# Storing the queries untransposed and reading them with a transposing DMA, with their rounding one half later and their products in four PSUM banks

## What is computed

```python
def _L0_xattn_ref(x, context, Wq, Wk, Wv):      # x is the layer-normed input, NHEADS = 32, HEAD_DIM = 32
    q = x @ Wq.T
    k_raw = context @ Wk.T
    v_raw = context @ Wv.T
    q = q.reshape(b, n, NHEADS, HEAD_DIM).transpose(0, 2, 1, 3)
    kv = jnp.concatenate([k_raw, v_raw], axis=-1).reshape(b, m, NHEADS, HEAD_DIM, 2)
    k, v = kv[..., 0].transpose(0, 2, 1, 3), kv[..., 1].transpose(0, 2, 1, 3)
    q, k = _rmsnorm(q), _rmsnorm(k)             # t * rsqrt(mean(t * t) + 1e-6) over the 32 of a head
    attn = softmax(einsum('bhnd,bhmd->bhnm', q, k) * HEAD_DIM ** -0.5)
    return einsum('bhnm,bhmd->bhnd', attn, v).transpose(0, 2, 1, 3).reshape(b, n, 1024)

x = x + tanh(g_xattn[0]) * _L0_xattn_ref(_layernorm(x), ctx_2048, Wq, Wk, Wv)
x = x + tanh(g_ffn[0]) * _L0_ffn_ref(_layernorm(x), w1, w2, w3)   # sigmoid(x Q(w1)') * (x Q(w2)'), then Q(w3)'
```

## Time and profile before

| | us |
|---|---|
| median of 3 runs (2406.19 to 2409.27) | 2406.49 |
| time of the profiled execution | 2409.68 |
| its span in the profile | 2407.9 |
| PE busy in the span | 2338.2 (97%) |
| DVE busy | 1423.5 (59%) |
| ACT busy | 1373.6 (57%) |
| POOL busy | 895.3 (37%) |

### The profile page before, as it was taken

The page is one execution under the profiler, slowest core; times in us unless marked ns, Lnnn a source line. Parts: engine busy times, 40 slices in busy tenths (PEclk is TensorE's granted clock), DMA queues, the critical chain, the costliest instruction groups (busy, mean ns, idle before and its releaser), DMA issues.

```text
span 2407.9 us, 46736 instructions
## 1 busy us (share of the span) xinstructions
PE 2338.2 (97%) x17618; PEld 1367.3 (57%) x17618; DVE 1423.5 (59%) x2346; ACT 1373.6 (57%) x2894; POOL 895.3 (37%) x857
## 2 busy tenths in 40 slices
PE   7998899999999999999999999889999999999999
PEld 5885465566656566666666565555555555544444
DVE  5666677776776777777767767664353444410000
ACT  4875787788888888888888888751111111110000
POOL 3664255565655656565656556430000000000000
PEclk9999999999999999999999999999999999999999
DMA  7785544465535445544545454554232323244351
GB/s 244 232 271 172 139 114 99 104 129 100 125 93 124 106 102 125 113 102 113 131 100 124 93 100 105 129 159 125 94 114 95 114 95 104 79 136 147 103 166 53
DMA packets 383233, 299.16 MB, mean 124 GB/s; under 512 B 276512, under 2 KB 338464, under 8 KB 382496
## 3 DMA queue, kind: packets, MB, share of 16 engines
q1 hardware_dynamic: 383008, 296.17, 46.8%
HBM read 196.22 MB, written 49.55 MB: 102 GB/s over the span
## 4 chain that ended last, share of the span: by engine, by line
PE 33%; POOL 29%; issue 26%; DVE 1%; DMA 1%; POOLq 1%; ACT 1%; DVEq 0%; SPq 0%; ACTq 0%
PE ps L1447 21%; POOL krs L707 14%; PE ps L1563 11%; POOL oinv L725 5%; POOL kms L702 4%; POOL osum L723 2%; POOL osum L730 2%; POOL oinv L727 1%; POOL ca L737 1%; POOL cn L751 1%; POOLq L60 0%; POOL crs L747 0%; DMA wraw<-in_wffn 0%; ACT pf L958 0%; DMA stage<-x_normalised 0%
## 5 line engine op out<-in xcount | busy, mean ns | idle before, releaser
L1479 PE MATMUL ps<-wk,cpair 128*128 128x512 f16 x4608 | 1116.5, 379 | 15.1 <-DVE cpair L1086 7.6
L1274 DVE TENSOR_TENSOR plo<-pf,phi 125x448 f16<-125x448 f32 x768 | 526.9, 687 | 160.8 <-ACT phi L949 158.4
L1479 PEld LDWEIGHTS ps<-wk,cpair 128*128 128x128 f16 x4608 | 393.7, 97 | 392.6 <-DVE cpair L1086 8.7
L958 ACT ACTIVATE pf<-ps 125x448 f32<-125x448 f32 x768 | 417.6, 544 | 145.1 <-PE ps L1501 137.1
L1447 PE MATMUL ps<-xnTh,w12q 128*128 128x512 f16 (+1 forms) x1408 | 478.9, 354 | 2.9 <-issue 2.1
L1447 PE MATMUL ps<-xnTl,w12q 128*128 128x512 f16 (+1 forms) x1408 | 478.6, 353 | 0.0
L949 ACT ACTIVATE phi<-pf 125x448 f16<-125x448 f32 x768 | 445.5, 580 | 8.5
L707 POOL TENSOR_TENSOR krs<-kms,mhalf 125x8 f32<-125x8 f32 x192 | 331.4, 1726 | 15.1
L702 POOL TENSOR_TENSOR kms<-kss,keps 125x8 f32<-125x8 f32 x192 | 95.5, 497 | 556.3 <-DVE kss L1240 556.3
L1525 PE MATMUL ps<-val,phi 125*128 125x65 f16 x3072 | 279.6, 192 | 18.9 <-DVE plo L1274 18.8
L1501 PEld LDWEIGHTS ps<-qT,kst 128*125 128x125 f16 x1536 | 209.2, 138 | 144.9
(11 more groups left out here) (113 smaller groups left out, 2461.0 us busy)
## 6 DMA issues: line engine op xcount, KB each, us to landing
gbuf<-in_wffn SPq DMA_DIRECT2D x66, 512.0 KB, 5.0
wraw<-in_wffn SPq DMA_DIRECT2D x66, 512.0 KB, 5.7
cstream<-in_ctx SPq DMA_DIRECT2D x48, 500.0 KB, 4.6
craw<-in_ctx SPq DMA_DIRECT2D x48, 500.0 KB, 4.6
hid<-hidden SPq DMA_DIRECT2D x7, 2816.0 KB, 12.7
hidden<-hh SPq DMA_DIRECT2D x66, 256.0 KB, 2.1
qT<-q_pairs SPq DMA_DIRECT2D x256, 56.0 KB, 2.2
wkraw<-in_wkv SPq DMA_DIRECT2D x4, 2048.0 KB, 8.9
```

The source lines that it names most:

```text
L958: act.activation(pf[0:KW, e % 6, :], bank(3 + e % 3)[0:KW, 0:2 * S], ACT.Exp, bias=LN128, scale=SCALE).then_inc(p_ready, 1)
L1274: dve.tensor_tensor(plo[0:KW, e % 6, :, :], pf[0:KW, e % 6, :].rearrange("p (t n) -> p t n", t=2), phi[0:KW, e % 6, :, :], ALU.subtract).t ...
L1479: mm = pe.matmul(bank(pt)[:, :], cpair[:, n % RING, a, kc, :], wkp[g][:, w, kc, :], start=(kc == 0 and m == 0), stop=(kc == KC - 1 and m = ...
```

## The change

- Q is stored untransposed, in `q_stacked` [token, head, 4, 32], with each head's high part twice and its low part twice. `half_high` and `half_low` therefore write 1024 elements for each row where they wrote 512, through a broadcast of `qhat`.
- `q_stack`, both `half_out` and the buffer `qTs` are gone. `save_q(h)` is one DMA of 512 KB straight from `qnat`. It waits for `qlo_ready`, and `half_high(h)` now waits for the DMA of half h - 2 (`q_saved`).
- `load_qT` is one transposing DMA from DRAM for each unit, 224 rows by 1024.
- `half_high(h)` stands behind `half(h + 1)` on ACT, `half_norm(h)` at the head of half h + 1 on DVE. `ctx_high(0)` stands behind `half(27)` and `half_high(26)`, `ctx_low(0)` behind `half_sums(27)` and `half_low(26)`. On SP `save_q(h)` stands in half h + 1, and so `save_q(0)` stands ahead of the third and fourth `cstream` loads.
- The products of half h go to bank (2, 3, 4, 6)[h % 4], and `q_half(h)` waits for `qhat_ready` of half h - 4.

```diff
+        def q_bank(h):
+            return (2, 3, 4, 6)[h % 4]
...
+            def save_q(h):
+                i, c = h // 2, h % 2
+                sp.wait_ge(qlo_ready, h + 1)
+                sp.dma_start(q_d[i * P:i * P + P, 16 * c:16 * c + 16, :, :].rearrange("t h a d -> t (h a d)"),
+                             qnat[:, c, :, :, :].rearrange("p h a d -> p (h a d)")).then_inc(q_saved[c], 16)
...
-                for i in range(4):
-                    for s in range(2):
-                        r0 = HD2 * s + DH * (i // 2)
-                        sp.dma_start(qT[DH * i:DH * i + DH, par, s:HG:2, :],
-                                     qst_d[g, :, r0:r0 + DH, b * S:b * S + S].rearrange("p r t -> r p t")
-                                     ).then_inc(q_in[par], 16)
+                sp.dma_start_transpose(qT[:, par, :, :], q_d[b * S:b * S + S, HG * g:HG * g + HG, :, :].rearrange(
+                    "t h a d -> t (h a d)")).then_inc(q_in[par], 16)
...
             def half_high(h, c):
                 act.wait_ge(qhat_ready, h + 1)
-                wait(act, qT_ready, h - 1)
-                act.activation(qnat[:, c, :, 0, :], qhat[:, :, :], ACT.Copy).then_inc(qhi_ready, 1)
+                wait(act, q_saved[c], 16 * (h // 2))
+                act.activation(qnat[:, c, :, 0:2, :], qhat[:, :, :].unsqueeze(2).to_broadcast([P, 16, 2, DH]), ACT.Copy
+                               ).then_inc(qhi_ready, 1)
...
                     half(h, c)
-                    if not first:
-                        half_out(h - 2, i - 1, c)
+                    if h:
+                        half_high(h - 1, 1 - c)
+                    if h == 2 * NT - 1:
+                        act.wait_ge(csc_ready, 1)
+                        ctx_high(0)
...
+                    if h:
+                        half_norm(h - 1, 1 - c)
+                    half_sums(h)
+                    if h:
+                        half_low(h - 1, 1 - c)
                     if h == 2 * NT - 1:
                         ctx_low(0)
...
             def q_half(h, i, par, c, first):
                 pe.wait_ge(xlo_ready, i + 1)
-                wait(pe, qhat_ready, h - 1)
+                wait(pe, qhat_ready, h - 3)
```

95 lines of the change are left out of this document (22 added, 73 removed).

## The result

| | before | after |
|---|---|---|
| median, us (lowest to highest) | 2407.26 (2406.19 to 2409.27, 4 runs) | 2385.66 (2383.76 to 2388.80, 4 runs) |
| profiled execution, its span | 2409.68, 2407.9 | 2383.76, 2381.9 |
| ratio of the times, 95% interval | | 0.9911 (0.9893 to 0.9928) |

The change is worth 21.6 us; 21.3 were forecast. The two profiles lie 26.0 us apart, since the profiled execution of before took 2.4 us more than its median and that of after 1.9 us less. They serve for the parts, and the medians for the sum. By the interval the medians' difference is uncertain by about 4 us.

The account below looks back on a forecast made before the run. PE was taken to bound the kernel. Terms 13.2 + 0.5 + 5.2 + 0.7 - 2.4 + 4.1 = 21.3 us, from 2406.49 to a forecast of 2385.2 us; range 2380.5 to 2393.5.

Parts of the forecast that it names:

- start, with the earlier x tile: Start of stage A: half 2 unstalled by four banks, x tile 2's transpose 5.2 us earlier, plus 0.7 for earlier x DMA.
- rest of stage A (13.2 + 0.5 - 2.4): Stage A: 13.2 us from removed stacks, 0.5 from a half no longer waiting for qhat, 2.4 lost before two weight sums.
- between the stages: From half 27 to the key tiles: second key tile earlier, low clock falling on the first key tile, 4.1 us gained.
- The stacks: Stage A: PE loses 25 stacks, 12 x 0.46 + 13 x 0.59 = 13.2 us; the tile becomes 11.75 us.
- ACT's and DVE's growth: Stage A: rounding grows to about 1.03 us, remainder to about 1.22; both fit, costed at zero outside tiles 3 and 9.
- The weight squares: Tiles 3 and 9: ACT's squares end late, PE waits 1.5 us instead of 0.3 before each weight sum, 2.4 us lost.
- The banks: Four banks for Q's products: no wait for qhat at the start, and 0.5 us for one later half.
- the banks do nothing: Rival at the start: xn of tile 2 comes later still, 5.9 us less gain, 2391; chance within another bound's 0.22.
- Stage B at zero: Stage B: one DMA for Q instead of 8 in each unit, unseen by PE, so no gain or loss.
- The transposing read: Stage B's read of Q from DRAM: 2.2 us to issue, 5.4 to landing, scaled from the key transpose.
- The rival of another bound in stage A: ACT, DVE or late DMAs hold most tiles at 12.3 us, or the clock falls: 2392; chance 0.22, banks' case included.
- sign of being wrong: Listed signs: tile near 12.8 us, PE waiting for xlo or xn, ACT waiting for q_saved, reads landing after 10 us.

Follow-up runs that it names:

- experiment 8: The kernel before, with each unit's first gate tile loaded ahead of the eight reads of Q on SyncE; 2397.53 us, 0.9956 of before.
- experiment 2: The changed kernel with eight dummy transposes of the identity into an unused bank behind each half in stage A; 2396.24 us, 0.9952 of before.
- experiment 3: The changed kernel with the squares of the two weight groups spread over more halves; 2381.47 us, 0.989 of before.
- experiment 1: The changed kernel with Q's products in two banks again, each half waiting for qhat of half h - 2; 2394.85 us, 0.995 of before.
- the repetition: The changed kernel run and profiled again, nothing altered, beside the kernel before; 2385.75 us, 0.991 of before.
- Experiments 6 to 9: Experiment 6: the changed kernel with 30 extra transposing reads of Q, ahead of the needed ones, 2397.81 us; experiment 7, experiment 8 and experiment 9 have their own lines.
- experiment 7: The changed kernel with 30 extra transposing reads of Q, each behind the needed read and the unit's first gate tile; 2384.88 us, 0.9906 of before.
- experiment 11: The changed kernel with spread squares, new step order between the stages, first gate tile ahead of Q, and clearing and tables ahead of half 27's norm; 2374.27 us.
- experiment 9: The changed kernel, with each unit's first gate tile loaded ahead of the transposing read of Q; 2380.57 us, 0.9889 of before.
- experiment 5: The kernel before, with the norm of half 0 ahead of the statistics of x tile 2 on DVE; 2404.21 us, 0.9988 of before.

## Why the prediction was right, and where only its sum was

| part of the sum | predicted us | in the two profiles |
|---|---|---|
| start, with the earlier x tile | 5.9 | 6.0 (40.85 to 34.88) |
| rest of stage A (13.2 + 0.5 - 2.4) | 11.3 | 8.6 (half 27 ends at 188.95, before at 203.54) |
| between the stages | 4.1 | 3.8 (to the first score) |
| stage B | 0 | 6.0 |
| behind stage B | 0 | 1.6 |
| sum | 21.3 | 26.0 |

**The start** was right in its steps: half 2 without a wait at full clock, and `xn` next in line with 0.64 us of idle time. It survived a first half that ran 0.94 us later in this execution (x transpose at 22.28). That the size fits so well is luck. The profile of before had a slow start, 2.3 us slower than experiment 8 with the same stage A, so the gain is 3.7 us against that one. The 0.7 us for an earlier x tile are not shown: its statistics stand at 29.62 instead of 30.35, but at 29.12 in experiment 8.

**The stacks** were right. The tile is 11.78 us against 11.75, and experiment 2 gives 1.05 us a tile. ACT's and DVE's growth was right too, 1053 and 1226 ns against 1.03 and 1.22 us, and outside the weight tiles PE shows no wait that comes from it.

**The weight squares** were under-sized. The mechanism was named, at 1.5 us a wait; the waits were 1.65 and 2.15, and the clock fell behind the second, which made the tile 1.7 us longer. I had taken from the earlier trace rows that the clock holds behind 2.46 us of idle. That the second wait is the longer one is the DMA of Q, which ACT waits for in that tile, 0.69 us; in the first such tile ACT idled 0.28 us there, for `qhat`. In all the term is 2.5 us short (0.15 + 0.65 + 1.7), and experiment 3 gets 4.2 back.

**The banks** were right at the start and wrong elsewhere. The text gave them the start's gain and 0.5 us; experiment 1 gives 9.1, of which 6.5 lie in stage A in the profiles, since a half without stacking comes back to its bank before `qhat` is ready. The rival "the banks do nothing" was far off. The sum didn't suffer, because it assumed PE unhindered in the tiles.

**Between the stages** the forecast of the first key product (4.3 us behind half 27, measured 4.24) was right, and that of the second key tile (12.3) became 12.8. The clock was low on the first key tile, as expected: 24 products in 7.04 us (8.1 in the text) in a stretch of 0.81. The 4.1 us of this term came out as 3.8 in the two profiles and as 1.7 in the repetition, whose clock fell once more, behind `khat`.

**Stage B at zero was wrong**, and this is the step that failed: "Between no change (bound below) and one unit's stall (above) I take zero". Two things were missing. One is the bound: eight issues replaced by one free SyncE for the rest of its list, 3.91 us against 1.56 ahead of the gate tiles of the fifth unit, so a gain was possible. The other is what stands behind the read on SyncE. I named the key transposes, not the gate tiles, though the waits view of before has DVE waiting 15.6 us for them. Experiments 6 to 9 show this, and the last two give its size: the gain of the changed kernel over before falls from 21.6 us to 17.0 (2397.53 against 2380.57) once both load the first gate tile ahead of Q. Stage B says the same in the profiles: 6.0 us shorter without that move and 1.4 with it (1321.0 against 1319.6). So about 4.6 us of the medians' 21.6 come from SyncE's list, and 17 from stage A and the passage between the stages, where 21.3 were forecast. The medians alone would not carry this split, since each of these differences is uncertain by 3 to 4 us. Two errors of about 4.5 us cancelled, and that the sum came within 0.3 us is luck.

**The transposing read** lands its 14 blocks in 4.9 us, 0.35 us a block, close to the estimate of 5.4 us. The estimate from the Trainium skill, page VectorE: DVE Perf Modes, The three transpose paths, was 18.3 us for it; this trace does not agree. Issue took 1.57 us against 2.2 estimated, and in experiment 7 30 more such reads cost nothing that the medians show.

The rival of another bound in stage A did not come, beyond the two waits for squares. But one sign of being wrong that the text names did: ACT waited for `q_saved`. DMA ran at a share of about 1.0 from 120 to 145 us in the changed kernel, and what came late in it was neither x nor context but the stored Q; through ACT's full list it reached PE at the second weight sum.

## What to carry to other kernels

A DMA costs its place in the issuing queue even if nobody waits for its data: read what stands behind it, and which engine's list waits for that. A wait of an engine that feeds the bound can cost its whole length though the bound's own gap right behind it shows less than half. It need not (the last one of experiment 8 cost 3.4 of 4.9 us), so compare the spacing of one repeated instruction ahead of the wait and far behind it. When a tile of the bound gets shorter, follow every chain that closes in it again (a bank, a sum of squares), for one that had slack before will now wait.

## What the hardware showed that I had not expected

The clock's fall does not follow the length of the idle time alone. Before the second weight sum PE idled 2.15 and 2.09 us in the two profiles of the changed kernel, and the eight transposes behind ran at about the lower level, 1.2 of 2.4 GHz (1.92 and 1.95 us instead of 1.03). Behind 2.93 us (experiment 1, half 2) PE kept the upper one, with a granted clock of 1.00. Even the same wait ends both ways. Behind 2.92 us for `khat` the next 54 products took 11.83 us at a clock of 1.00 in experiment 2, and 13.39 us at 0.88 in experiment 11. Behind 1.65 us before the first weight sum the clock was 1.00 in the changed kernel and fell in experiment 9, to 0.51 from 73.0 to 76.3 us.

The fall can also come when PE is busy again: about 1.0 us behind the end of a wait of 2.21 us (experiment 5, half 2) and of 3.20 us (experiment 8, half 2), where the clock was 0.94 and 0.96 in the first microsecond, and then 0.50 (30.7 to 34.0 us) and 0.51 (32.4 to 35.8). So a look at the first products behind a wait does not tell whether the clock held. No run here separates what made the difference.

The 1.6 us behind stage B lie where no code was changed. PE waits there for a DMA of `stage`, 4.79 us at 1632.19 before and 3.14 us at 1606.21 after, and the whole stretch took 816.4 and 814.8 us; it took 815.9 in the repetition.

A transposing read from DRAM of 224 rows by 1024 columns held SyncE for 1.4 to 4.8 us (median 1.57), longer than the key transpose's 1.23, and it landed in 4.3 to 6.9 us, beside a stream of other loads.
